# One-hot matrices of the slot maps: a share of the rows built by ScalarE, multiplied in smaller pieces, and a shorter source list

## The reference

```
h = tokens(x)                                  # patches -> 37 tokens a sequence
h = concat(h, txt)                             # 16 x 165 x 256
h = h + selective_scan(layernorm(h))
h = h + experts0(layernorm(h))                 # 4 groups of 2 experts; each token takes its best group
h = h + attention(layernorm(h))                # rotary, causal
h = h + experts1(layernorm(h))                 # 4 experts; each token takes the best 2
return h
```

## Time and profile before

| | us |
|---|---|
| median of 3 executions | 867.62 (865.6 to 869.97) |
| the profiled execution | 870.52 |
| its span in the trace | 868.7 |
| PE busy | 770.0 (89% of the span) |
| DVE busy | 513.6 (59%) |
| ACT busy | 361.6 (42%) |
| POOL busy | 366.0 (42%) |

### The profile page before, as it was taken

The page is one execution under the profiler, slowest core; times in us unless marked ns, Lnnn a source line. Parts: engine busy times, 40 slices in busy tenths (PEclk is TensorE's granted clock), DMA queues, the critical chain, the costliest instruction groups (busy, mean ns, idle before and its releaser), DMA issues.

```text
span 868.7 us, 17549 instructions
## 1 busy us (share of the span) xinstructions
PE 770.0 (89%) x5506; PEld 606.8 (70%) x5507; DVE 513.6 (59%) x1252; ACT 361.6 (42%) x806; POOL 366.0 (42%) x314
## 2 busy tenths in 40 slices
PE   3998923999999999869999999949999999999991
PEld 2767911666666666557777776838999989999981
DVE  4896989433333434268887877864555555555550
ACT  5796662333333333324433332514444444444430
POOL 2449941132323222214556651022555555555542
PEclk9996975999999999969999996959999999999996
DMA  9950044141121212161121223401333333323325
GB/s 257 415 225 2 1 148 138 20 110 30 25 35 24 36 24 31 16 209 50 50 67 55 55 66 105 165 27 31 50 49 49 49 49 49 49 49 49 43 26 149
DMA packets 37748, 66.75 MB, mean 77 GB/s; under 512 B 3872, under 2 KB 29840, under 8 KB 36144
## 3 DMA queue, kind: packets, MB, share of 16 engines
q1 hardware_dynamic: 23696, 46.90, 16.4%
q0 software_dynamic: 13824, 19.01, 14.2%
q10 hardware_dynamic: 192, 0.38, 0.1%
HBM read 45.23 MB, written 23.74 MB: 79 GB/s over the span
## 4 chain that ended last, share of the span: by engine, by line
PE 76%; DVE 14%; ACT 4%; DMA 2%; issue 1%; POOL 0%; POOLq 0%; SPq 0%; DVEq 0%
PE PS L905 15%; PE PS L713 15%; PE PS L918 15%; PE PS L731 7%; PE PS L1230 5%; PE PS L721 2%; PE PS L1271 2%; PE PS L1226 2%; PE PS L1261 2%; PE PS L1263 2%; DVE tops L660 2%; PE PS L1243 1%; PE PS L1234 1%; DMA Y<-in_wtok_dram 1%; PE PS L891 1%
## 5 line engine op out<-in xcount | busy, mean ns | idle before, releaser
L1057 POOL DMA_INDIRECT sum<-X,dest x48 | 97.9, 2040 | 107.0 <-ACT X L972 94.9
L713 PE MATMUL PS<-X,Y 128*128 x576 | 134.7, 384 | 1.2 <-DVE Y L811 1.2
L918 PE MATMUL PS<-X 128*128 x768 | 133.5, 273 | 1.8 <-ACT X L972 1.8
L905 PE MATMUL PS<-X 128*128 128x256 f16 x768 | 130.7, 276 | 1.5 <-DVE X L990 1.5
L962 ACT ACTIVATE X<-PS,X 128x256 f32<-128x256 f32 x192 | 75.2, 474 | 110.7 <-PE PS L905 110.7
L905 PE MATMUL PS<-X,Y 128*128 128x256 f16 x384 | 105.8, 276 | 0.0
L918 PE MATMUL PS<-Y,X 128*128 x384 | 104.7, 273 | 0.0
L822 DVE SCALAR_TENSOR_TENSOR Y<-PS,Y 128x512 f32<-128x512 f32 x48 | 36.1, 751 | 112.4 <-PE PS L713 112.4
L877 POOL DMA_INDIRECT sum<-Y,dest x24 | 38.0, 1585 | 148.2 <-ACT Y L788 148.2
L713 PEld LDWEIGHTS PS<-X,Y 128*128 128x128 f16 x576 | 56.9, 99 | 60.8 <-issue 4.3
L905 PEld LDWEIGHTS PS<-X 128*128 x768 | 75.8, 99 | 11.4 <-issue 2.1
(11 more groups left out here) (363 smaller groups left out, 1480.5 us busy)
## 6 DMA issues: line engine op xcount, KB each, us to landing
X<-in_w_dram SPq DMA_DIRECT2D x11, 1024.0 KB, 15.9
stage<-in_w_dram SPq DMA_DIRECT2D x16, 512.0 KB, 3.5
sum<-h SPq DMA_DIRECT2D x2, 2048.0 KB, 7.5
xs<-Y SPq DMA_DIRECT2D x2, 1040.0 KB, 5.1
xs<-Y SPq DMA_DIRECT2D x2, 1032.0 KB, 6.3
h<-in_txt_dram SPq DMA_DIRECT2D x2, 1024.0 KB, 18.7
Y<-in_patches_dram SPq DMA_DIRECT2D x3, 672.0 KB, 9.2
sum<-h SPq DMA_DIRECT2D x2, 768.0 KB, 3.9
```

The source lines that it names most:

```text
L713: ins = nc.tensor.matmul(PS[:, 2 * u + s, 0:F0], x_[:, slot, k, :], w_[:, at_:at_ + F0], start=(n == 0), stop=(n == 3 * KC - 1))
L905: ins = nc.tensor.matmul(PS[:, 2 * s + c // 2, (c % 2) * T1:(c % 2 + 1) * T1], part[:, off:off + P], x_[:, slot, k, :], start=(n == 0), st ...
L918: ins = nc.tensor.matmul(PS[:, 4 + a, 0:D], h_[:, s, c, a * P:(a + 1) * P], part[:, off:off + D], start=(s == 0 and c == 0 and n == 0), st ...
L1057: nc.gpsimd.indirect_dma_start(out=sum1, out_offset=bass.IndirectOffsetOnAxis(ap=dest[:, i:i + 1], axis=0), in_=y1buf[:, i // 2 % 2, i % 2 ...
```

## The change

- `inrow` is built by two engines. ACT builds the rows of the first 6 of 22 columns in layer 0 and of the first 12 of 44 in layer 1 (`ACT_ROWS`): per column |k_iota - row| over 128 elements (Abs with the negated row as bias, into `nearly`, which lies in `stage`), then over all of them at once Relu(1 - that), which is 1 where the two are equal and 0 elsewhere. It does so behind the last `norm_row`.
- DVE builds the rest, in 2 pieces of 8 columns in layer 0 and 3 pieces of 11, 11 and 10 in layer 1 (`PIECES`). `pe_slots` waits once for ACT's columns (`act_hot`) and for DVE's first piece, then for each further piece.
- The slot number is masked with -128 instead of shifted by 7 and is compared as it is, an integer, with `slot_at` (128 x `k_slot`). The row, also an integer, is compared with `k_iota`. The two casts to float are gone, and a negation into `minus` for ACT is new.
- `k_tile` holds 0 to 21 twice, so no token number has to lose `TOKENS`. `source` is written by the second operation after the products, and `from_` is formed again for `dest`.
- POOL prepares `slot_at` and the second half of `k_tile` at the start. The counts of `pads_zeroed` and `routes_in` go on `consts_ready` and `petab_ready`, in the same order of the same instructions.

```diff
+PADS, PETAB = 4, 5
+ACT_ROWS = (6, 12)
+PIECES = (2, 3)
...
+        minus = rc[:, 2 * TOPK:3 * TOPK, :]
+        slot_at = sb("slot_at", [P, SLOT1])
+        nearly = stage[:, 0, :].bitcast(BF16).rearrange("p (c n) -> p c n", n=P)
...
+        def row_pieces(done):
+            first, last = ACT_ROWS[done], (1 + done) * NT
+            step = -(-(last - first) // PIECES[done])
+            return [(c, min(c + step, last)) for c in range(first, last, step)]
+
+        def act_rows(act, done, inrow):
+            act.wait_ge(rows_known, done + 1)
+            n = ACT_ROWS[done]
+            column = minus.rearrange("p c t -> p (c t)")
+            for c in range(n):
+                nc.scalar.activation(nearly[:, c, :], k_iota, ACT.Abs, bias=column[:, c:c + 1]).then_inc(act_hot, 1)
+            act.wait_ge(act_hot, sum(ACT_ROWS[0:done + 1]) + done)
+            nc.scalar.activation(inrow[:, 0:n, :], nearly[:, 0:n, :], ACT.Relu, bias=1.0, scale=-1.0).then_inc(act_hot, 1)
...
         def pe_slots(pe, done, n, tiles, inrow, intile):
+            pieces = [c for c, _ in row_pieces(done)]
+            earlier = done * len(row_pieces(0))
+            pe.wait_ge(act_hot, sum(ACT_ROWS[0:done + 1]) + done + 1)
+            pe.wait_ge(hot_ready, earlier + 1)
             for i in range(n):
-                if i % (n // 2) == 0:
-                    pe.wait_ge(hot_ready, 2 * done + i // (n // 2) + 1)
+                if i in pieces:
+                    pe.wait_ge(hot_ready, earlier + pieces.index(i) + 1)
...
+            row_of, first_of = low7[:, 0:choices, :], high7[:, 0:choices, :]
             chain.link(nc.vector.tensor_copy(pos[:, 0:choices, :], slots_of))
-            chain.link(nc.vector.tensor_scalar(low7[:, 0:choices, :], pos[:, 0:choices, :], P - 1, None, ALU.bitwise_and))
-            chain.link(nc.vector.tensor_scalar(high7[:, 0:choices, :], pos[:, 0:choices, :], 7, None,
-                                               ALU.logical_shift_right))
+            chain.link(nc.vector.tensor_scalar(row_of, pos[:, 0:choices, :], P - 1, None, ALU.bitwise_and))
+            nc.vector.tensor_scalar(minus[:, 0:choices, :], row_of, -1.0, None, ALU.mult).then_inc(rows_known, 1)
+            chain.link(nc.vector.tensor_scalar(first_of, pos[:, 0:choices, :], -P, None, ALU.bitwise_and))
...
-            half = n // 2
-            for c0 in (0, half):
-                nc.vector.tensor_tensor(inrow[:, c0:c0 + half, :], each(slots_of, P)[:, c0:c0 + half],
-                                        along(k_iota, P)[:, c0:c0 + half], ALU.is_equal).then_inc(hot_ready, 1)
+            for c0, c1 in row_pieces(done):
+                nc.vector.tensor_tensor(inrow[:, c0:c1, :], each(row_of, P)[:, c0:c1],
+                                        along(k_iota, P)[:, c0:c1], ALU.is_equal).then_inc(hot_ready, 1)
...
             chain.link(nc.vector.tensor_copy(from_, row_))
-            chain.link(nc.vector.scalar_tensor_tensor(out=place, in0=tile_, scalar=float(P), in1=from_, op0=ALU.mult,
+            nc.vector.scalar_tensor_tensor(out=source[:, 0:tiles], in0=tile_, scalar=float(P), in1=from_, op0=ALU.mult,
+                                           op1=ALU.add).then_inc(source_ready, 1)
+            dve.wait_ge(source_ready, done + 1)
+            chain.link(nc.vector.scalar_tensor_tensor(out=from_, in0=tile_, scalar=float(P), in1=from_, op0=ALU.mult,
                                                       op1=ALU.add))
-            chain.link(nc.vector.tensor_scalar(from_, place, float(TOKENS), -float(TOKENS), ALU.is_ge, ALU.mult))
-            chain.link(nc.vector.tensor_tensor(from_, from_, place, ALU.add))
-            nc.vector.tensor_copy(source[:, 0:tiles], from_).then_inc(source_ready, 1)
-            dve.wait_ge(source_ready, done + 1)
             dest_of_token(dve, chain, tiles, from_, to, taken)
...
             for t in range(2, NT):
                 norm_row(t)
+            act.wait_ge(w0_split, XW // CW)
+            act_rows(act, 0, inrow0)
             act_experts0(act)
...
             for t in range(6, NT):
                 norm_row(t)
+            act.wait_ge(stage_free, AHEAD + W1W // CW)
+            act_rows(act, 1, inrow1)
             act.wait_ge(c_psum, 3)
...
+            nc.gpsimd.tensor_scalar(slot_at[:, :], k_slot, float(P), None, ALU.mult)
+            nc.gpsimd.tensor_copy(k_tile[:, NT:TOPK * NT], k_tile[:, 0:NT])
```

More of the change, by code:

```diff
@@ L380, in build @@
         consts_ready = sem("consts_ready")
-        pads_zeroed = sem("pads_zeroed")
+        rows_known = sem("rows_known")
         dve_done = sem("dve_done")
@@ L442, in build @@
         amax_ready = sem("amax_ready")
-        routes_in = sem("routes_in")
+        act_hot = sem("act_hot")
         prep_copied = sem("prep_copied")
@@ L572, in dest_of_token @@
         def dest_of_token(dve, chain, tiles, from_, to, taken):
-            dve.wait_ge(consts_ready, 5 + SG)
+            dve.wait_ge(consts_ready, PADS + 3 + SG)
             chain.link(nc.vector.tensor_tensor(to, spare[:, 0:tiles], taken, ALU.mult))
@@ L613, in positions @@
             chain.link(nc.vector.tensor_tensor(slots_of, slots_of, k_far.unsqueeze(1).broadcast_to([P, choices, NT]), ALU.add))
+            row_of, first_of = low7[:, 0:choices, :], high7[:, 0:choices, :]
             chain.link(nc.vector.tensor_copy(pos[:, 0:choices, :], slots_of))
-            chain.link(nc.vector.tensor_scalar(low7[:, 0:choices, :], pos[:, 0:choices, :], P - 1, None, ALU.bitwise_and))
-            chain.link(nc.vector.tensor_scalar(high7[:, 0:choices, :], pos[:, 0:choices, :], 7, None,
-                                               ALU.logical_shift_right))
+            chain.link(nc.vector.tensor_scalar(row_of, pos[:, 0:choices, :], P - 1, None, ALU.bitwise_and))
+            nc.vector.tensor_scalar(minus[:, 0:choices, :], row_of, -1.0, None, ALU.mult).then_inc(rows_known, 1)
+            chain.link(nc.vector.tensor_scalar(first_of, pos[:, 0:choices, :], -P, None, ALU.bitwise_and))
             n = choices * NT
-            chain.link(nc.vector.tensor_copy(slots_of, high7[:, 0:choices, :]))
             each = lambda ap, m: ap.rearrange("p c t -> p (c t)").unsqueeze(2).broadcast_to([P, n, m])
             along = lambda ap, m: ap.unsqueeze(1).broadcast_to([P, n, m])
-            chain.link(nc.vector.tensor_tensor(intile[:, :, 2, :], each(slots_of, tiles), along(k_slot[:, 0:tiles], tiles),
+            chain.link(nc.vector.tensor_tensor(intile[:, :, 2, :], each(first_of, tiles), along(slot_at[:, 0:tiles], tiles),
                                                ALU.is_equal))
-            chain.link(nc.vector.tensor_copy(slots_of, low7[:, 0:choices, :]))
             nc.vector.tensor_tensor(intile[:, :, 0, :], intile[:, :, 2, :],
@@ L641, in positions @@
             tile_, row_, taken = (PS[:, 7, i * tiles:(i + 1) * tiles] for i in range(3))
-            place, from_, to = (tok[:, i, 0:tiles] for i in range(3))
+            from_, to = (tok[:, i, 0:tiles] for i in (1, 2))
             chain.link(nc.vector.tensor_copy(from_, row_))
-            chain.link(nc.vector.scalar_tensor_tensor(out=place, in0=tile_, scalar=float(P), in1=from_, op0=ALU.mult,
+            nc.vector.scalar_tensor_tensor(out=source[:, 0:tiles], in0=tile_, scalar=float(P), in1=from_, op0=ALU.mult,
+                                           op1=ALU.add).then_inc(source_ready, 1)
+            dve.wait_ge(source_ready, done + 1)
+            chain.link(nc.vector.scalar_tensor_tensor(out=from_, in0=tile_, scalar=float(P), in1=from_, op0=ALU.mult,
                                                       op1=ALU.add))
-            chain.link(nc.vector.tensor_scalar(from_, place, float(TOKENS), -float(TOKENS), ALU.is_ge, ALU.mult))
-            chain.link(nc.vector.tensor_tensor(from_, from_, place, ALU.add))
-            nc.vector.tensor_copy(source[:, 0:tiles], from_).then_inc(source_ready, 1)
-            dve.wait_ge(source_ready, done + 1)
             dest_of_token(dve, chain, tiles, from_, to, taken)
@@ L1775, in _ @@
             nc.gpsimd.memset(onesf[:, :], 1.0).then_inc(consts_ready, 1)
[L1777 to L1780, removed]
+            nc.gpsimd.memset(xT[:, :, BATCH * SEQ:], 0.0).then_inc(consts_ready, 1)
+            pool.wait_ge(consts_ready, 3)
+            nc.gpsimd.memset(h[96:P, BATCH:NT, :], 0.0).then_inc(consts_ready, 1)
+            pool.wait_ge(consts_ready, PADS)
             nc.gpsimd.memset(groups[:, :], 0.0).then_inc(consts_ready, 1)
-            pool.wait_ge(consts_ready, 3)
+            pool.wait_ge(consts_ready, PADS + 1)
             for g in range(SG):
                 nc.gpsimd.memset(groups[32 * g:32 * g + 32, g:g + 1], 1.0).then_inc(consts_ready, 1)
-                pool.wait_ge(consts_ready, 4 + g)
+                pool.wait_ge(consts_ready, PADS + 2 + g)
             pool.sem_inc(stage_free, 2)
@@ L1802, in _ @@
             pool.wait_ge(wsm_loaded, 16)
-            nc.gpsimd.tensor_copy(wbcd_pad, wr0).then_inc(routes_in, 1)
```

(13 more changed lines are left out.)

2 lines of the change are left out of this document (1 added, 1 removed).

## The result

The change took 860.90 us (median of 6 executions, 859.98 to 861.85) beside 868.33 for the kernel before (6 executions, 864.18 to 870.20): ratio 0.9924, 95% interval 0.9899 to 0.9949, so 6.6 us faster by the ratio, 4.4 to 8.8 by the interval. Timed a second time, against 23 executions of before on the same chip, it was 0.9938 (0.9921 to 0.9956), 5.4 us. Forecast were 862.6 us and -5.0.

The account below looks back on a forecast made before the run. It took layer 0's routing as bound by DVE alone, layer 1's by DVE's first piece, its second, then PE. Terms -1.1 (layer 0) and -3.9 (layer 1) sum to -5.0, from 867.62 to 862.6 us; range 859.6 to 866.0.

Parts of the forecast that it names:

- DVE: Before the products: casts save 0.32 us, fewer columns more; expert list 1.1 earlier in layer 0, 1.85 in layer 1.
- The tail: DVE's operations behind the slot products fall from nine to seven: -0.43 us in layer 0, -0.46 in layer 1.
- ACT: ACT's columns at 0.38 us an Abs: done at 137.5 in layer 0, setting PE's start; covered in layer 1.
- my lower bound: An Abs at 0.25 us: in layer 0 DVE's expert list decides, and the gain is 1.5 us.
- PE in layer 0: 22 slot products take some 1.5 us, from 137.55 to 139.05; with the operations behind them -1.1.
- PE in layer 1: Slot products without a gap at full clock, -4.3 us, less 0.4 for a fall towards the end: -3.9.
- The gather: Layer 0: source list 1.3 us earlier, at 139.5, when the last stored rows have landed; the gather stays covered.
- the cover I had named: Layer 0: ACT's copy of the first tile, done at 144.5, stays ahead of DVE's maxima, ending at 144.9.
- rival 4: Stored rows or the gather end last in layer 0, so its gain is lost: -3.9 us, 863.7; chance 0.10.
- Half clock in the slot products of layer 1: Layer 1 gains only 2.1 us, -3.2 in all: 864.4; chance 0.27.
- An Abs at 0.50: ACT's columns come late: layer 0 gives -0.4 us, layer 1 still -3.9: 863.3; chance 0.09.
- Integer operands: Integer comparisons slow DVE in both layers, so it ends last: +3.5 us together, 871.1; chance 0.04.

Follow-up runs that it names:

- a2: The change again, unedited, against the kernel before: ratio 0.9938 (0.9921 to 0.9956).
- b4: The change with layer 1's first tile split, transposed and started ahead of the bound: 858.30 us, ratio 0.9892 to the kernel before.
- c2: The same kernel as b4, timed once more: 859.07 us, ratio 0.9906 to the kernel before.
- c3: b4 with 14 instead of 12 of layer 1's columns on ACT: 858.47 us, ratio 0.9899 to the kernel before.
- b1: The kernel before with only POOL's two start operations and the moved semaphore counts: 867.38 us beside 867.30, ratio 1.0001.
- a4: The change with DVE's share in one piece per layer instead of two and three: ratio 0.9996 to the kernel before.
- a1: The kernel before, unedited, against itself: ratio 1.0003 (0.9988 to 1.0019).
- b2: The kernel before with only the shorter source list, seven operations behind the products instead of nine: ratio 0.9992 to the kernel before.
- c1: The change with every Abs of ACT's share done twice, once into an unread place: 866.52 us, ratio 0.9985 to the kernel before.
- a3: The change without ACT's share, all columns on DVE in pieces of 11: ratio 0.9932 to the kernel before, from 5 executions.
- b3: The same kernel as a3, timed once more: ratio 0.9964 to the kernel before, from 12 executions.

## Why the prediction was right, and where it was off

The measured -6.6 (and -5.4 the second time) stands for a forecast of -5.0, with faster as the likeliest; the time, 860.9, lies in the range. By its steps:

- **DVE, right.** From the first operation on row numbers to the first piece it was 2.49 in layer 0 (133.17 to 135.66) and is 2.14 (130.02 to 132.16), -0.35 for the -0.32 I had for the casts. Pieces of 1024 elements took 1.218 us (predicted 1.22), and in layer 0 the first piece came 1.64 behind the first comparison, as computed (133.70 to 135.34 there, 130.52 to 132.16 here). The tail is 1.55 (135.42 to 136.97) for 1.90 in layer 0, -0.35 for the -0.43 I had; in layer 1, up to the start of the last cast, it is 1.45 (561.74 to 563.19) for 1.89 (572.09 to 573.98), -0.44 for -0.46. Shifted to the scale of the trace before by that first operation on row numbers, the lists start at 138.6 in layer 0 and 568.2 in layer 1, where I had 139.1 and 568.3.
- **ACT, mis-sized.** I had 0.38 an Abs, worked out from whole durations. It shows 0.386 of duration, but the operations start 0.29 apart (six in 1.84, the last one 0.39 long), since they overlap. Six of them and the Relu are done 0.5 earlier than I had it, and layer 0 gave 1.4 to 1.5 (21.2 and 21.0 for 22.5), my lower bound's 1.5, and not 1.1. The prediction had PE's products end 0.45 behind DVE's list of experts; they end 0.05 ahead of it. The ends that I kept, 0.25 and 0.50, held it. The Trainium skill's budget ("ScalarE: Activation LUTs", Rules for kernel authors), 0.41 an operation, is farther off still for operations that overlap like these.
- **PE in layer 0, right in its length and start:** 22 products in 1.50; and ACT does set its start, as the earlier trace rows suggested. With the faster ACT its end no longer decides.
- **PE in layer 1, right at its upper end.** Forecast: full clock from the first product, 34 in a row, ten behind the last piece, -4.3 with the tail, less 0.4 for a fall. Measured against the first profile: 30.3 for 34.7, -4.4. No fall came in these products, in any of the five profiles with the full change or more (the change, a2, b4, c2, c3). But a third of that was luck: where the kernel before has its products at full clock, the gain is 33.3 - 30.3 = 3.0. So the -3.9 that I took for layer 1 lies between the two by accident rather than for my reason.
- **The gather, right in the first profile, with the cover I had named, and short of cover in two others.** POOL now waits for the stored rows and not for the list, as rival 4 had it, but in the first profile they cost nothing: ACT's copy of the tile is done at 140.90 and DVE's maxima end at 141.36.

```profile
136.76 1.19 POOL L891 DMA_INDIRECT Y<-xs,source  x1 [20.48 <-DMA xs<-Y]
...
140.52 0.38 ACT L793 ACTIVATE Y<-PS 128x256 f16<-128x256 f32 x1 [6.69 <-PE PS L725]
...
141.38 0.42 DVE L834 TENSOR_TENSOR Y<-PS,Y 128x256 f16<-128x256 f32 x1
```

In the second profile of the change (a2) the rows landed later, POOL began its gather 1.5 us behind the list instead of 0.9, and DVE stood 0.26 us for ACT's copy:

```profile
139.63 1.19 POOL L891 DMA_INDIRECT Y<-xs,source  x1 [21.02 <-DMA xs<-Y]
...
143.88 0.42 DVE L834 TENSOR_TENSOR Y<-PS,Y 128x256 f16<-128x256 f32 x1 [0.26 <-ACT Y L793]
```

In b4 it stood 0.45 us. So rival 4 comes true in part in some executions, and a still shorter routing of layer 0 would meet this path next.

- **The rivals.** Half clock in the slot products of layer 1 came in no profile of the change. An Abs at 0.50 was not seen. Integer operands cost nothing: 128x1408 took 1.614 for 1.618.
- **The rest.** Routings that are 5.9 shorter (1.4 to 1.5 and 4.4) against a before at half clock, 4.5 against one at full, bracket the timed 5.4. The first timing's 6.6 lies 0.7 above the larger of them, which is inside its interval. b1 shows nothing from the start of the kernel, but can't exclude 0.7. What remains I take for scatter; that is argued, not shown.

## What to carry to other kernels

Cut a producer into pieces so that the consumer never has to stop: a4 against the change is the same work on the same engines, 5 us apart. Price short operations by the distance of their starts, not by their durations, and before lending an idle engine a share, find the wait in front of which it will stand: its room was 0 in one layer and 2.5 us in the other. When two profiles differ by more than the edit can explain, cut both at instructions that they share before explaining anything.

## What the runs showed of the hardware beyond what was expected

TensorE's clock does not follow its pauses at once. It fell 0.2 us after the last of a run of one-row f32 products in the first profile of before, at the beginning of a pause of 1.26; not at all over the same pause in a1 and in b1; and in a4 only some 2.8 us after the last product, when PE was already working again (from 558.88, the end of the one-row products, to about 561.7). The Trainium skill ("TensorE: Matmul & The Clock Gate", Part 1) has the monitor run free of the kernel, and the trace agrees: one kernel, both outcomes. It also says that pauses are what brings the clock down, and there the runs go with it in the plain sense only: without a pause it did not fall in five profiles (the change, a2, b4, c2, c3); with a pause of over 1 us it fell in four (before, b2, a4, c1) and not in two (a1, b1). In three of the four (before, b2, c1) it fell within 0.2 to 0.4 us of the last one-row product, so the length of the pause can't have brought that fall, and what did is not shown. In a3 and b3 pauses of 0.7 us among the slot products did not bring the clock down.
